# Moving the last tap of a depthwise convolution from ScalarE and GpSimd to a VectorE instruction that reads PSUM

## What is computed

```python
xn = layernorm(x)
xz = einsum('bsd,ed->bse', xn, W_in)              # 1024 outputs: x_inner and z, 512 each
x_inner, z = split(xz, 2)
conv = depthwise_conv(x_inner, conv_w, 4 taps, causal) + conv_b
x_conv = silu(conv)
s_C = (x_conv @ W_x.T)[..., 16:]
h = scan: h = 0.95 * h + x_conv                   # over the tokens
y = h * (s_C @ exp(B_log).T) * silu(z)
resid = xn + y @ W_out.T
out = x + layernorm(resid) * ln_g + ln_b + mx_linear(xn, weight, bias)
```

## Time and profile before

| | before |
|---|---|
| median of 3 runs | 267.05 us (265.92 to 267.52) |
| profiled execution, its own time | 264.35 us |
| its span (first to last instruction) | 262.5 us |
| PE busy | 212.7 us, 81% |
| DVE busy | 226.2 us, 86% |
| ACT busy | 157.9 us, 60% |
| POOL busy | 205.9 us, 78% |
| largest wait of ACT: SiLU (line 644) for line 395 on POOL | 29.9 us |
| largest wait of POOL: line 395 for the taps on DVE | 13.9 us |

### The profile page before, as it was taken

One profiled execution on the slowest core, in us unless ns is written; L12 is line 12 of the kernel. 1 busy time (PEld: TensorE's weight loads), 2 busy tenths in 40 slices (PEclk: granted clock), 3 DMA queues, 4 the chain that ended last, 5 costly groups with the idle time before them and its releaser, 6 DMA issues.

```text
span 262.5 us, 3471 instructions
## 1 busy us (share of the span) xinstructions
PE 212.7 (81%) x1252; PEld 175.5 (67%) x1252; DVE 226.2 (86%) x304; ACT 157.9 (60%) x240; POOL 205.9 (78%) x131
## 2 busy tenths in 40 slices
PE   0459954887699999879999969979999898667960
PEld 0438833355589887668898918868988587557960
DVE  3799899998599899958999999598999999683455
ACT  2897391466956537657995347748966444555450
POOL 1328949999997789999689599999597989995262
PEclk9989998599999999999999979999999999959995
DMA  6965000000000000004112000000202000002204
GB/s 223 289 199 160 1 2 0 0 1 0 0 2 0 1 2 0 0 0 152 47 48 80 0 0 1 2 0 2 80 0 82 1 0 0 0 2 80 84 0 160
DMA packets 10777, 11.18 MB, mean 43 GB/s; under 512 B 648, under 2 KB 10120, under 8 KB 10760
## 3 DMA queue, kind: packets, MB, share of 16 engines
q1 hardware_dynamic: 9488, 9.96, 11.6%
q10 hardware_dynamic: 1272, 0.99, 1.4%
HBM read 6.76 MB, written 4.19 MB: 42 GB/s over the span
## 4 chain that ended last, share of the span: by engine, by line
POOL 35%; DVE 25%; PE 12%; ACT 11%; issue 10%; DMA 5%; POOLq 0%; ACTq 0%; DVEq 0%
POOL hy L403 12%; POOL xc L395 8%; POOL rstd L383 6%; DVE xc L997 5%; DVE hy L1026 4%; DMA y<-fx 3%; DVE fx L1076 3%; DVE y_lo L1046 3%; PE slot L754 2%; POOL xd L425 2%; ACT xn L595 2%; DVE bn L934 2%; DVE rs L1061 2%; PE obank L857 2%; PE obank L850 2%
## 5 line engine op out<-in xcount | busy, mean ns | idle before, releaser
L758 PE MATMUL slot<-xn_hi,w_in_lo 128*128 128x512 f32 x128 | 52.8, 412 | 8.5 <-DVE xn_lo L986 3.3
L395 POOL TENSOR_TENSOR xc<-xc,tap 128x1021 f32<-128x1021 f32 x16 | 46.1, 2881 | 13.9 <-DVE xc L997 13.9
L403 POOL TENSOR_TENSOR hy<-hy,sz 128x1024 f32<-128x1024 f32 x16 | 48.9, 3058 | 3.6 <-DVE hy L1026 2.3
L759 PE MATMUL slot<-xn_lo,w_in_hi 128*128 128x512 f32 x128 | 51.3, 401 | 0.0
L760 PE MATMUL slot<-xn_hi,w_in_hi 128*128 128x512 f32 x128 | 51.1, 399 | 0.0
L1026 DVE TENSOR_TENSOR_SCAN hy<-decay,xc 128x1024 f32<-128x1024 f32 x16 | 45.4, 2844 | 0.7 <-ACT xc L644 0.7
L997 DVE SCALAR_TENSOR_TENSOR xc<-slot,cw,xc 128x1023 f32<-128x1023 f32 (+1 forms) x32 | 40.2, 1265 | 1.6 <-ACT tap L632 1.1
L758 PEld LDWEIGHTS slot<-xn_hi,w_in_lo 128*128 128x128 f32 x128 | 24.5, 191 | 20.7 <-issue 4.7
L644 ACT ACTIVATE xc<-xc 128x1024 f32<-128x1024 f32 x16 | 17.0, 1060 | 29.9 <-POOL xc L395 29.9
L849 PE MATMUL obank<-w_out_lo,y_hi 128*128 128x256 f32 x128 | 32.0, 282 | 0.0
L850 PE MATMUL obank<-w_out_hi,y_hi 128*128 128x256 f32 x128 | 32.0, 282 | 0.0
(11 more groups left out here) (106 smaller groups left out, 525.8 us busy)
## 6 DMA issues: line engine op xcount, KB each, us to landing
y<-fx SPq DMA_DIRECT2D x7, 512.0 KB, 2.9
x_in<-L_attn_x SPq DMA_DIRECT2D x3, 1024.0 KB, 5.6
x_in<-L_attn_x SPq DMA_DIRECT2D x2, 512.0 KB, 4.0
rs<-L_attn_W_in SPq DMA_DIRECT2D x2, 512.0 KB, 10.0
fx<-L_attn_W_out SPq DMA_DIRECT2D x1, 512.0 KB, 12.5
y<-fx SPq DMA_DIRECT2D x2, 256.0 KB, 2.1
fx<-L_ffn_weight ACTq DMA_DIRECT2D x1, 256.0 KB, 7.8
xc<-L_attn_B_log ACTq DMA_DIRECT2D x1, 256.0 KB
```

What stands on the lines that cost most here:

```text
L395: pool.tensor_tensor(xc[:, c, TAPS - 1:], xc[:, c, TAPS - 1:], tap0[:, c % 2, 0:n], ALU.add).then_inc(conv_ready, 1)
L403: pool.tensor_tensor(hy[:, c, :], hy[:, c, :], sz[:, :], ALU.mult).then_inc(hsz_ready, 1)
L758: pe.matmul(dst, w_lo, m_hi, start=first, stop=False)
L759: pe.matmul(dst, w_hi, m_lo, start=False, stop=False)
```

## The change

The tile `tap0` goes, with ScalarE's write of it and GpSimd's addition. `conv_tap0` becomes a VectorE operation, the same `scalar_tensor_tensor` as for taps 2 and 1, with the slot shifted by 3 columns. It stands right behind `conv_tap1` of its chunk, four places in a step. `taps_ready` counts one per chunk instead of two, and TensorE's waits for a free slot go from `tap1_done` to `conv_ready`, as VectorE now reads the slot once more.

```diff
             @of_batch
-            def conv_tap0(b, c):
-
-                wait(pool, tap1_done, NCH * b + c + 1)
-                n = SEQ - (TAPS - 1)
-                pool.tensor_tensor(xc[:, c, TAPS - 1:], xc[:, c, TAPS - 1:], tap0[:, c % 2, 0:n],
-                                   ALU.add).then_inc(conv_ready, 1)
...
             def step(s):
                 prev, here, nxt = s - 1, s, s + 1
-                conv_tap0(here, 2)
-                conv_tap0(here, 3)
                 gate(here, 1)
...
                 rstd_2(prev, 1)
-                conv_tap0(nxt, 0)
                 scale_g(prev, 1)
-                conv_tap0(nxt, 1)
                 gate(nxt, 0)
...
                                scale=cw[:, c, TAPS - 1:TAPS]).then_inc(taps_ready, 1)
-
-                wait(act, conv_ready, NCH * b + c - 1)
-                act.activation(tap0[:, c % 2, :], src, ACT.Copy, scale=cw[:, c, 0:1]).then_inc(taps_ready, 1)
...
-                slot_free(nxt, (tap1_done, NCH * nxt + 1, nxt))
+                slot_free(nxt, (conv_ready, NCH * nxt + 1, nxt))
                 z_half(nxt, 0)
                 out_tile(here, 2)
-                slot_free(nxt, (tap1_done, NCH * nxt + 2, nxt))
+                slot_free(nxt, (conv_ready, NCH * nxt + 2, nxt))
                 x_half(nxt, 3)
...
-                wait(dve, taps_ready, 2 * (NCH * b + c + 1))
+                wait(dve, taps_ready, NCH * b + c + 1)
                 conv_tap(b, c, TAPS - 2, tap2_done)
...
+            @of_batch
+            def conv_tap0(b, c):
+                wait(dve, tap1_done, NCH * b + c + 1)
+                conv_tap(b, c, TAPS - 4, conv_ready)
...
                 conv_tap2(here, 2)
                 aggregate(nxt, 0)
                 conv_tap1(here, 2)
+                conv_tap0(here, 2)
                 conv_tap2(here, 3)
                 conv_tap1(here, 3)
+                conv_tap0(here, 3)
                 mean_var(nxt, 0)
                 scan(here, 1)
...
                 conv_tap2(nxt, 0)
                 conv_tap1(nxt, 0)
+                conv_tap0(nxt, 0)
                 block_scale(nxt, 1)
                 take_tile(here, 0)
                 conv_tap2(nxt, 1)
                 conv_tap1(nxt, 1)
+                conv_tap0(nxt, 1)
```

More of the change, by code:

```diff
@@ L125, in build @@
         xd_lo = sb("xd_lo", [P, KM, SEQ], F32R)
-        tap0 = sb("tap0", [P, 2, SEQ])
         xc = sb("xc", [P, NCH, SEQ])
@@ L390, in conv_tap0 @@
             @of_batch
-            def conv_tap0(b, c):
-                wait(pool, tap1_done, NCH * b + c + 1)
-                n = SEQ - (TAPS - 1)
-                pool.tensor_tensor(xc[:, c, TAPS - 1:], xc[:, c, TAPS - 1:], tap0[:, c % 2, 0:n],
-                                   ALU.add).then_inc(conv_ready, 1)
-            @of_batch
             def gate(b, c):
@@ L909, in step @@
                 z_half(nxt, 2)
-                slot_free(nxt, (tap1_done, NCH * nxt + 3, nxt))
+                slot_free(nxt, (conv_ready, NCH * nxt + 3, nxt))
                 s_product(nxt)
-                slot_free(nxt, (tap1_done, NCH * nxt + 4, nxt))
+                slot_free(nxt, (conv_ready, NCH * nxt + 4, nxt))
                 z_half(nxt, 3)
```

## The result

The changed kernel took 285.51 us (median of 4 runs, 284.49 to 287.67) against 267.28 us (265.92 to 267.52) for the kernel before on the same chip: a ratio of 1.0732, with a 95% interval of 1.0685 to 1.078. The forecast was 280, in a range from 272 to 286; on the 267.05 us from which it started, the ratio makes 286.6, just above the range. The sign and most of the mechanism came out as forecast; the sum did not: 13.2 us were added up, and the ratio makes it 19.5 us of 267.

What follows compares the result with a forecast made beforehand. VectorE, busiest at 86%, and its lock with GpSimd were taken to bound the kernel. Terms 2.0 + 2.1 + 1.0 + 2.4 + 2.2 + 2.4 + 1.1 = 13.2 us gave 277.6 profiled, median 280; range 272 to 286.

Steps and rivals of the forecast that it cites:

- stretch B: From half 0's last addition to the next convolution of chunk 2: +2.4 us at each of the two later borders.
- batch 3: Last turn, from the convolution of chunk 2 through scans 1 and 2 and the quantisations: +1.1 us.
- 2.4 without a gap: In the last turn, both quantisations run back to back in 2.4 us behind scan 2, with gate 2 following them.
- The border 0 to 1: Between batches 0 and 1, without an fx addition: two taps of 1.25 less a 0.4 wait for TensorE, +2.1 us.
- xn_low's wait: VectorE's wait in front of xn_low, near output tile 7, should shrink from 2.7 to about 1.4 us.
- The time between two scans 1: The turn from one batch's scan 1 to the next one's should grow by 4 to 5 us.
- TensorE's slots at nothing: Releasing TensorE's slots by tap 0 instead of tap 1 costs nothing; otherwise up to 1.25 us at four uses per turn.
- All on the path: Rival: nothing is hidden, all 16 taps cost their full 1.25 us, 20 us in all, 287 us; chance 0.08.
- Faster: Rival: GpSimd's chain of waits is right, ten pieces of 2 us become taps of 1.25, -8.5, 258.6 us; chance 0.07.
- GpSimd sets stretch A: Rival: from chunk 2's convolution to output tile 7, GpSimd's earlier gate 1 gives -1.3 per turn; +2.7 overall, 270; chance 0.10.
- Absorbed: Rival: VectorE's idle time takes up 3.0 of each turn's 5.0 us and lock collisions fall otherwise; 273 us; chance 0.13.

Runs made afterwards that it cites:

- without any tap 0: The changed kernel with tap 0 of the convolution left out altogether, on any engine: 261.56 us, ratio 0.9843 to the kernel before.
- chunks 0 and 1 alone: The kernel before with tap 0 moved to VectorE for chunks 0 and 1 only: 275.91 us, ratio 1.0396.
- the late slots: The kernel before with only TensorE's four waits for a free slot asking for conv_ready instead of tap1_done: 270.46 us, ratio 1.0175.
- tap 0 twice: The changed kernel with VectorE's tap 0 instruction issued a second time for every chunk: 304.4 us, ratio 1.1425 to the kernel before.
- the fx addition moved: The changed kernel with the addition of half 1 into fx in front of scan 0 instead of behind it: 282.03 us, ratio 1.0626.
- the block scale moved at the late borders: The changed kernel with half 1's block scale ahead of chunk 0's taps, only at the two borders where GpSimd scales a finished half: 280.95 us, ratio 1.0578.
- both quantisations moved: The changed kernel with both quantisations directly behind scan 2, ahead of the next batch's statistics: 283.11 us, ratio 1.0646.
- all three together: The changed kernel with the fx addition, late-border block scale and both quantisations all moved forward: 277.08 us, ratio 1.0431.

## Why the prediction was right and where it failed

The forecast sign, the lock between VectorE and GpSimd and the pieces that were walked through it were right; the sum came out 6 us short, at the two steps named below.

**The lock held, step by step.** Every duration that was walked through the lock in the turn of batch 2 came within 0.3 us, and the fill from the first tap on, batches 0, 1 and 2 and the fx addition at the border fit to 0.2. Batch 3 and the block scale are the exceptions. VectorE with two SBUF operands stands for a whole GpSimd instruction and the other way round; taps from PSUM stand for nothing (1254 to 1281 ns on average in all three shapes).

**The step that failed first: stretch B, +2.4 where +4.5 was measured, twice.** The prediction followed the scans and additions through that stretch as those held by the lock, and passed over the block scale, which has one SBUF operand and 32 columns and took 0.17. So its cost was put at what it had been in its old place, though the one of half 0 took 0.73 in the same trace. Moving it by one tap put it behind GpSimd's scaling by g, 2.04 us at either border, 4.1 us in the sum; with the block scale moved forward the time fell by 4.1. The removed addition did not have to be there to keep the two apart (0.17 without any tap 0); the extra tap did it, with ScalarE's input to the scaling ready 0.6 sooner. That with the input as late as before the block scale would have passed at 3.9 is read from the rows and was not tried. The order rows ahead of the prediction show the block scale (L951) behind the third tap and GpSimd's scaling (L445) behind nothing but small operations. The Trainium skill, "SBUF — State Buffer", section "Who interferes with whom", names `tensor_scalar` among the operations that can enter the mode that takes the shared port; the rows 2.21 and 2.12 agree. The section also says that a VectorE instruction with at most one SBUF input stays clear of GpSimd only outside that mode. The prediction took over the two-operand case and the sentence on one input without this condition, which may be why it did not look at the block scale.

**The second: batch 3, +1.1 where +2.5 was measured.** "2.4 without a gap" was the step: gate 2, issued 0.16 us after the first quantisation had begun, ran between the two. The kernel before had shown this: the pair of scans of batch 0 took 6.22, because GpSimd's addition, issued 0.02 after the first had begun, ran between them:

```profile
41.81 4.05 POOL L395 TENSOR_TENSOR xc<-xc,tap 128x1021 f32<-128x1021 f32 x1 [0.51 <-DVE xc L997]
```

The same two scans kept the lock in the changed kernel (4.47 for both), with gate 1 issued only when scan 1 ended. Who was waiting when the first of the pair ended seems to decide; that was read from these rows and not tried by itself.

**The sum with both put in:** 13.2 + 4.1 + 1.4 = 18.7 us, beside 19.5 by the ratio, and beside 19.0 in the profiled pair (21.7 less the 2.0 ahead of the first tap and the 0.7 of the next paragraph).

**The border 0 to 1, +2.9 for +2.1,** was forecast right, and 0.7 of it is TensorE's clock in this execution. TensorE's two products in front of output tile 0 took 7.2 us where they took 5.7, at a lower granted clock. The stretch table of the kernel after (span, busy us of PE, PEld, DVE, ACT, POOL, then the granted clock):

```profile
74.00:81.20 7.20, 7.20 (x24) 5.74 (x25) 7.17 (x7) 3.79 (x4) 7.20 (x3) 0.76 0.00 0
75.30:78.20 2.90, 2.90 (x8) 2.29 (x7) 2.90 (x3) 1.27 (x2) 2.90 (x3) 0.50 0.00 0
```

and of the kernel before:

```profile
70.00:75.70 5.70, 5.68 (x24) 4.54 (x25) 5.70 (x6) 5.70 (x6) 5.70 (x3) 1.00 0.00 0
```

Within these 7.2 us the granted clock was 0.50 from 75.3 to 78.2, which is 1.2 GHz, and 2.4 GHz ahead of it and behind it. The same products take 7.2 us in three other executions (chunks 0 and 1 alone, the late slots, tap 0 twice) and 5.7 in the other eight. Among the eight are the fx addition moved, the block scale moved at the late borders, both quantisations moved and all three together, which have the changed kernel's order at this border: there it takes 13.5 us in all four, +2.1 over the 11.4 before, and 14.2 here. TensorE had stood idle for the same 1.98 us in front of the products in runs of either kind; what lowers the clock is not shown.

**The quantisation of batch 2, its neighbours and xn_low.** Quantisation 0 took 2.88 (forecast near 3), the fx addition 2.95 (2.8), GpSimd 153.6 us busy (160). VectorE's busy time was forecast at 246 and is 253.7; the waits inside the lock, which the page counts as busy, were sized too small (4.1 of the difference is the block scale). xn_low's wait shrank from 2.73 to 0.18 instead of 1.4. That mark failed by 1.2 although the 2.2 us it was to bear witness to came out as 2.1. The time between two scans 1 grew by 2.5, 6.9 and 6.6 us, not by 4 to 5; the last two have the block scale in them.

**TensorE's slots at nothing.** Right for this change, as VectorE never waits for ScalarE's taps. The prediction's reason, that the slot's next user is queued later anyway, was not the whole of it: TensorE does wait, 5.1 us in three places. By the rows what hides it is the slack between TensorE's product and VectorE's next tap, and the late slots used that up (VectorE then waits 3.8 us for ScalarE's taps, 1.1 before).

**The rivals.** "All on the path" (287) was nearer to the measured time than the forecast, for another reason than it gave: batches 0 to 2 did absorb part of their taps, and collisions took its place. "Faster" was the reading by the chain of waits: without any tap 0 its 21 us were 4.2. "GpSimd sets stretch A" fell with xn_low's wait, which vanished. "Absorbed" fell at the borders: the wait in front of xn_low was used up and a turn still cost 3.8, 5.7 and 6.6 us.

## What to carry to other kernels

When an operation moves by a microsecond against another engine's queue, walk every neighbour through the lock, the tiny ones too: here an instruction of 0.17 us took 2.2 as soon as a long one of the other engine started in front of it. Walk every turn, the last one too: the moved fx addition gained at two borders and lost 1.6 in the tail. Ask also what starts earlier once an instruction is gone. The share of a line in the chain of waits is no bound on what its removal brings (21 us in the chain, 4.2 us measured), but leaving the work out in one run tells it at once.

## What the hardware showed beyond that

The lock passes between engines in the middle of a back-to-back pair: GpSimd's gate, waiting since 0.16 us after the first of two quantisations began, ran before the second (the pair 4.48 us, the gate 3.25). A VectorE operation from SBUF on 128x32 elements is held until GpSimd's instruction on 128x1024 ends (2.21 and 2.12 us behind its multiplication by g and its y_lo, 0.85 and 0.73 where it came near their end), while the powers of GpSimd on four columns hold nothing on VectorE in the rows seen here, but are themselves held by it (3.00 us beside scan 2 for a bare 1.0). TensorE's granted clock over the same two products was 0.76 in the changed kernel's execution and 1.00 in others with the same order there.
